# The heads stage: running maxima by broadcast loads, masks on the pool, and 32-row scores of four heads

## The reference, cut to what matters

```
log_f_cum = cumsum(log_sigmoid(fg))              # per head, along the sequence
log_D     = tril(log_f_cum[s] - log_f_cum[t]) + ig[t]      # -inf above the diagonal
D         = exp(log_D - max_t log_D)
C         = (q k^T / sqrt(32)) * D
h         = C / (max(|sum_t C|, exp(-max log_D)) + eps) @ v
out       = layernorm of h over each head's 32 features, times ln_scale
```

## Time and profile before

| | us |
|---|---|
| median of 3 runs | 1692.03 |
| lowest, highest | 1690.22, 1693.12 |
| the profiled execution's own time | 1693.99 |
| its span | 1692.3 |
| busy: TensorE, its weight loads, VectorE, ScalarE, pool | 1453.1, 1217.1, 922.0, 711.7, 357.9 |

### The profile page before, as it was taken

How to read it: one execution, slowest core, us unless ns; L and a number is a source line. 1 busy time by engine, 2 the same in 40 slices (tenths; PEclk the granted TensorE clock), 3 DMA queues, 4 the chain that set the end, 5 groups by cost and what they waited for, 6 DMA issues and landing times. The chain is left out here.

```text
span 1692.3 us, 27012 instructions
## 1 busy us (share of the span) xinstructions
PE 1453.1 (86%) x7570; PEld 1217.1 (72%) x7571; DVE 922.0 (54%) x1622; ACT 711.7 (42%) x1612; POOL 357.9 (21%) x253
## 2 busy tenths in 40 slices
PE   6999865998999996896999881499995899999977
PEld 5888732887888875775788650477885788888866
DVE  3222256558586877443444326733335977777774
ACT  3111134355555554512555541344444466666620
POOL 0111110104040310061862007111017900000004
PEclk8999988999999997698999995699996999999989
DMA  8763663954453543144664567732224455555402
GB/s 311 272 236 113 235 202 113 272 167 155 139 178 124 180 137 128 60 168 156 190 188 130 173 221 224 212 125 113 110 112 141 134 167 153 168 154 165 112 32 100
DMA packets 161503, 273.58 MB, mean 162 GB/s; under 512 B 28896, under 2 KB 63968, under 8 KB 157600
## 3 DMA queue, kind: packets, MB, share of 16 engines
q1 hardware_dynamic: 135920, 207.39, 38.7%
q10 hardware_dynamic: 17664, 38.68, 5.9%
q0 software_dynamic: 7856, 26.74, 4.7%
HBM read 162.00 MB, written 106.57 MB: 159 GB/s over the span
## 5 line engine op out<-in xcount | busy, mean ns | idle before, releaser
L2314 ACT ACTIVATE attend_prob<-banks,attend_row,rq 128x128 f32<-128x128 f32 x256 | 113.7, 454 | 70.1 <-DVE attend_row L2364 70.1
L1962 DVE TENSOR_TENSOR queries_total<-queries_total,queries_sq 128x512 f32<-128x512 f32 x64 | 44.3, 693 | 129.2 <-ACT queries_sq L1933 129.2
L100 PE MATMUL banks<-heads_split,heads_wl 128*128 (+1 forms) x256 | 109.4, 427 | 2.7 <-DVE heads_wt L744 2.7
L100 PE MATMUL banks<-of_x_lead,queries_wl 128*128 128x512 f32 x256 | 101.2, 395 | 7.7 <-ACT queries_sq L1933 4.4
L100 PE MATMUL banks<-attend_wol,attend_ol 128*128 (+1 forms) x256 | 106.7, 417 | 0.0
L100 PE MATMUL banks<-values_wl,of_ctx_lead 128*128 128x512 f32 x256 | 100.9, 394 | 4.3 <-DVE values_wt L2098 4.3
L101 PE MATMUL banks<-heads_split,heads_wl 128*128 (+1 forms) x256 | 103.0, 402 | 0.0
L102 PE MATMUL banks<-heads_split,heads_wt 128*128 (+1 forms) x256 | 102.6, 401 | 0.0
L102 PE MATMUL banks<-attend_wol,attend_ot 128*128 (+1 forms) x256 | 101.0, 395 | 0.0
L102 PE MATMUL banks<-of_x_lead,queries_wt 128*128 128x512 f32 x256 | 100.7, 393 | 0.0
L101 PE MATMUL banks<-attend_wot,attend_ol 128*128 (+1 forms) x256 | 100.7, 393 | 0.0
(11 more groups left out here) (306 smaller groups left out, 3880.7 us busy)
## 6 DMA issues: line engine op xcount, KB each, us to landing
v_heads<-values_out SPq DMA_DIRECT2D x16, 1024.0 KB, 4.8
heads_raw<-in_L_xattn_ki_w SPq DMA_DIRECT2D x32, 512.0 KB, 3.9
k_heads<-heads_key ACTq DMA_DIRECT2D x64, 256.0 KB, 3.1
q_heads<-queries_head ACTq DMA_DIRECT2D x16, 1024.0 KB, 3.9
attend_q<-q_heads SPq DMA_DIRECT2D x64, 256.0 KB, 4.1
of_attend_k<-k_heads SPq DMA_DIRECT2D x60, 256.0 KB, 4.0
of_attend_v<-v_heads SPq DMA_DIRECT2D x60, 256.0 KB, 3.3
sorted_rows<-values_zeros SPq DMA_DIRECT2D x2, 5120.0 KB, 19.9
```

The lines of the kernel that those rows point to most:

```text
L100: nc.tensor.matmul(out, lead_l, lead_r, start=first, stop=False)
L1962: nc.vector.tensor_tensor(t, t, sq[:, n % 2, :], ALU.add).then_inc(acc_done, 1)
L2314: ins = nc.scalar.activation(prob[:, j % 2, b, :], ps[:, j % 2, b * S:(b + 1) * S], ACT.Exp, bias=row[:, j % 2, 1, b:b + 1], scale=rq[:, b ...
```

## The change

- The running maxima g go to DRAM as they are made (four stores at the end of `gates`); the copy into `M.g` and the rest L328 are gone.
- In the heads stage SyncE loads g for two heads at a time, broadcast over the 128 partitions (`load_g`, 512 KB), into a ring of four. The pool writes 1e30 above the diagonal (`mask`), five units ahead. ScalarE's `exp` works out exp(a - g) by itself, four instructions of 128x128, each with a column of `M.nat` as bias. `maxima` and `argument` are gone, and with them `pick`, `far` and `ident_b`, `arg`, and two banks of PSUM.
- `qz` with its zeros (and their memset, L771) is replaced by `q`, one load for four heads. `scores` runs once in four steps, for four heads, each in its own 32 rows and its own bank.
- The pool's big steps are cut in four pieces each and placed between the masks; VectorE's two reductions and ScalarE's square are cut in two. ScalarE does `pair` first in a step, VectorE `decayed` first, TensorE `keys` first.

Core of the diff:

```diff
+            for g in range(G):                                   # gates, SyncE
+                sp.wait_ge(m_done, g + 1)
+                sp.dma_start(g_dram[g * H0 * N:(g + 1) * H0 * N].rearrange("(h n) -> h n", n=N),
+                             grow[0:H0, g * N:(g + 1) * N]).then_inc(g_stored, 16)
...
+            def load_g(g, k):
+                sp.dma_start(gmax[:, k % 4, :], g_dram[bass.ds((g * PAIRS + k) * 2 * N, 2 * N)]
+                             .partition_broadcast(P)).then_inc(g_ring[k % 4], 16)
+            load_g(0, 0), load_kT(0, 0), load_q(0, 0), load_g(0, 1), load_ctx(0)     # then kT, q,
+            ...                               # load_g(0, 2), load_g(0, 3), lnb, load_raw(0)
+            sp.wait_ge(qk, 4)
+            load_q(0, 2)                      # then load_split(0), load_raw(1), kbias, body(0)
...
+                    if n % 2 == 0:                               # body, SyncE
+                        sp.wait_ge(dec_done, g * PER + n + 2)
+                        load_g(g if k < PAIRS - 4 else after(g, PER)[0], (k + 4) % PAIRS)
...
+            def mask(g, n):                                      # pool
+                pool.wait_ge(g_ring[h // 2 % 4], (g * (PAIRS // 4) + n // 8 + 1) * 16)
+                nc.gpsimd.affine_select(out=t, in_=t, compare_op=ALU.is_ge, fill=FAR, base=0,
+                                        pattern=[[0, GB], [1, S]], channel_multiplier=-1).then_inc(masked, 1)
+            def body(g, first):
+                for n in range(PER):
+                    mask(g, n + AHEAD)
+                    if 5 <= n < 8: ...                           # pieces of values
+                        for at, step in ((3, centre), (8, scale), (10, weigh), (12, add)):
...
             def exp(g, n, first):                                # ScalarE
-                act.wait_ge(arg_done, g * PER + n + 1)
+                act.wait_ge(masked, g * PER + n + 1)
-                nc.scalar.activation(dec[:, n % 2], arg[:, n % 2], ACT.Exp).then_inc(dec_done, 1)
+                for b in range(GB):
+                    ins = nc.scalar.activation(dec[:, n % 2, b], gmax[...], ACT.Exp, scale=-1.0,
+                                               bias=M.nat[:, 0, bass.ds(g1, 1), b, h:h + 1]...)
+                ins.then_inc(dec_done, 1)
...
             def scores(g, n, first):                             # TensorE
-                nc.tensor.matmul(ps[:, 4 + n % 2, s], kT[:, c, s], qz[:, c % 2, j, s], ...)
+                if not (first and n < 4):
+                    pe.wait_ge(c_done, g * PER + n)
+                for b in range(GB):
+                    for j in range(4):
+                        ins = nc.tensor.matmul(ps[:, 2 + j, s], kT[r, c % C, s], q[r, c % 2, s], ...)
...
-                    maxima(g, n + 2, first)
-                    scores(g, n + 2, first)
                     lagging(g, n - LAG, keys)
+                    if n % 4 == 2:
+                        scores(g, n + 2, first)
                     outputs(g, n, first)
```

More of the change, by code:

```diff
@@ L375, in heads_and_keys @@
     LAG = 8
+    AHEAD = 5
     UNITS = PER * G
@@ new lines, in value @@
+            def value(g, count, b):
+                if b == 0:
+                    pool.wait_ge(loaded_ctx, (count + 1) * 16)
+                    if not isinstance(g, int) or g > 1:
+                        pool.wait_ge(pv, (count - 1) * PER)
+                    ph.hold(pool, held_pool)
+                ins = nc.gpsimd.tensor_copy(ctx1[:, bass.ds(half(g), 1), b, :, 0:DH0].rearrange("p a h e -> p (a h) e"),
+                                            ctx[:, b, :].rearrange("p (h e) -> p h e", e=DH0))
+                if b == GB - 1:
+                    ins.then_inc(ctx1_done, 1)
@@ new lines, in weigh, with add @@
+            def weigh(g, b):
+                if b == 0:
+                    pool.wait_ge(norm_done, FIRST + g + 1)
+                    ph.hold(pool, held_pool)
+                out = piece(sq, b).rearrange("p h e -> p (h e)")
+                ins = nc.gpsimd.tensor_tensor(out, out, lnb[:], ALU.mult)
+                if b == GB - 1:
+                    ins.then_inc(scale_done, 1)
+            def add(g, b):
+                if b == 0:
+                    pool.wait_ge(scale_done, g + 1)
+                    ph.hold(pool, held_pool)
+                xg = K.x[:, bass.ds(g * GB + b, 1), :].rearrange("p a d -> p (a d)")
+                ins = nc.gpsimd.tensor_tensor(xg, xg, piece(sq, b).rearrange("p h e -> p (h e)"), ALU.add)
+                if b == GB - 1:
+                    ins.then_inc(res_done, 1)
@@ new lines, in body @@
+            def body(g, first):
+                for n in range(PER):
+                    mask(g, n + AHEAD)
+                    if 5 <= n < 8:
+                        for b in ((0,), (1, 2), (3,))[n - 5]:
+                            value(after(g, PER)[0], g + 1, b)
+                    if not first:
+                        for at, step in ((3, centre), (8, scale), (10, weigh), (12, add)):
+                            if at <= n < at + 2:
+                                step(g - 1, 2 * (n - at))
+                                step(g - 1, 2 * (n - at) + 1)
@@ L571, in _ @@
+            for n in range(2):
+                mask(0, n)
+            for b in range(GB):
+                value(0, 0, b)
+            for n in range(2, AHEAD):
+                mask(0, n)
             nc.gpsimd.memset(total[:], 0.0).then_inc(total_blank, 1)
             pool.wait_ge(loaded_w, 16)
-            values(1, 1)
+            body(0, True)
             with pool.Fori(1, G) as g:
[L575 to L588, removed]
-                own(nc.gpsimd.tensor_tensor(out, out, lnb[:].unsqueeze(1).broadcast_to([P, GB, D]), ALU.mult))
-                xg = K.x[:, bass.ds((g - 1) * GB, GB), :]
-                nc.gpsimd.tensor_tensor(xg, xg, out, ALU.add).then_inc(res_done, 1)
@@ L658, in body @@
                 for n in range(PER):
-                    lagging(g, n - LAG + 1, weight_lead)
-                    exp(g, n + 2, first)
-                    lagging(g, n - LAG - 1, keep_key)
                     if n % 2 == 0:
@@ L666, in body @@
                             pair(g - 1, PAIRS - 1)
+                    lagging(g, n - LAG + 1, weight_lead)
+                    exp(g, n + 2, first)
+                    lagging(g, n - LAG - 1, keep_key)
                     if not first:
@@ L687, in _ @@
                 if m == PER - LAG + 3:
-                    square(last)
+                    square(last, 0)
+                    square(last, 1)
                 if m == PER - LAG + 6:
@@ L789, in _ @@
             finish(PER - LAG + 1)
-            mean(last)
+            mean(last, 0)
+            mean(last, 1)
             dve.wait_ge(mean_done, G)
-            shift(nc.vector, last)
+            for b in range(GB):
+                ins = shift(nc.vector, last, b)
+            ins.then_inc(centred, 1)
             for m in range(2, 5):
                 finish(PER - LAG + m)
-            variance(last)
+            variance(last, 0)
+            variance(last, 1)
             for m in range(5, 7):
```

253 lines of the change are left out of this document (122 added, 131 removed).

## The result

The changed kernel takes 1652.07 us (median of 4, 1649.65 to 1656.8) where the kernel before takes 1692.57 (4 runs): 0.9762 of it, 95% interval 0.9734 to 0.979. The forecast was 1644, its range 1622 to 1674. The profiled execution took 1652.70 us, its span is 1651.0.

What follows compares the result with a forecast made beforehand. TensorE was taken to bound the heads stage: 56 steps of 4.40 instead of 5.41 us (-56.6), a later start (+6.7) and loads catching up (+2) sum to -47.9, from 1693.99 to 1646.1, as a median 1644; range 1622 to 1674.

Steps and rivals of the forecast that it cites:

- TensorE bounds the stage; the step shrinks by what leaves it: Heads stage: TensorE sets the pace; its own step becomes 4.13 us, the whole step 4.40 instead of 5.41.
- Scores, 2.0 us for four heads: TensorE's scores in four row groups: half overlapped, 2.0 us per four heads, 0.55 a step with 0.05 for array shape changes.
- side by side in full: Rival on TensorE's scores: full overlap, TensorE 3.83, step 4.15, 14 us less, 1630; chance 0.10.
- The rest of the step: TensorE's step without scores: keys 2.66 and outputs 0.92 stay, 3.58 us; 0.05 for changing the array's shape.
- Stalls, 0.27 a step: Added to TensorE's 4.13 us step: table loads on ScalarE and collisions of pool, VectorE and loads, 4.3 us per 16 steps.
- ScalarE: ScalarE's step in the heads stage: four exponentials 1.14 us, 3.7 us of work in all, 85% busy, 10% under TensorE.
- ScalarE becomes the bound: Rival: four exponential instructions take 1.8 to 1.9 us, ScalarE 4.4, step 4.7, 17 us more, 1661; chance 0.18.
- VectorE and Pool: Heads stage: VectorE 2.9 us a step, pool 1.9, 0.4 charged for blocking; no 128x512 VectorE instruction above 2 us.
- DMA: Heads stage: broadcasts add 256 KB, 0.8 us a step; engines 3.4 of 4.4 us, share near 0.77.
- the 8 that would have sunk it: Sign against the forecast: broadcasts taking over 8 us to land in the steady part.
- Start: Start of keys in the heads stage: about 329 instead of 322.30, 6.7 us later, behind loads and the fifth broadcast.
- the loads that catch up in group 0: Group 0 of the heads stage: a further 2 us lost while loads catch up.

Runs made afterwards that it cites:

- the 1618 us kernel: Changed kernel with raw weights loaded ahead of ctx, the pair's copy last in ScalarE's step, and the group loop written out on four engines: 1618.40 us, ratio 0.956.
- the run from the same rows: The 1618 us kernel with the scores of all four heads taken from rows 0 to 31 instead of each head's own rows: 1710.13 us, ratio 0.9974.

## Why the prediction was right, step by step

- *TensorE bounds the stage; the step shrinks by what leaves it.* Right. The floor is 3.98 (forecast 4.13), and the 1618 us kernel, at 4.06, shows that it is one.
- *Scores, 2.0 us for four heads.* Too dear: 1.11. The rival "side by side in full" had it, and the run from the same rows shows the cause. The reason I gave for half, that the two passes of a matmul share their rows, didn't hold, as 1.11 us is near the 1.01 of full overlap; how the passes lie over each other no row shows. Worth 0.22 x 56 = 12 us, in the kernel's favour. The rest of the step was too cheap: 3.70 us where I had 3.58 and the 0.05 for changing the array's shape, for which I had no row. 4 us against.
- *Stalls, 0.27 a step.* This is the term that failed: 0.67, 22 us more. I priced table loads and collisions, but not ScalarE's order (`pair` first), nor raw's place behind 1 MB, nor the loop's turn. The three together are 287.00 - 254.54 = 32.5 us, 0.58 a step. Of the three, only raw's place is as it was before, where L635 waited for TensorE alone and never for the load. `pair` first is the change's own, and the trace of before has no stall at the turn. The disturbed steps that it does have, 4.75 and 3.19 us of idle TensorE the longest, are VectorE's behind Pool, and they went as forecast.
- *ScalarE.* Four exponentials take 1.26 to 1.28, forecast 1.14; its work is 175.59 / 240 x 4.65 = 3.40 a step, forecast 3.7, and it was 73% busy, not 85. The rival "ScalarE becomes the bound" is wrong as a sum of work: taking 0.56 us a step off it gave 1.3 us where nothing held it up. The four instructions for one did cost, by way of the hold-ups: with one instead, 20.8 us went, by lead or, at the turns, by shorter code.
- *VectorE and Pool.* Right: L797 fell from 1186 to 944 ns, and the whole Pool steps bring the long blocks back. No L797 took over 1.79 us. The masks do hold VectorE up, as the 1003 and 890 ns with and without them show, and were held up themselves (781 ns in the mean, 0.63 us the shortest); they cost the stretch nothing.
- *DMA.* Share 0.68 to 0.76 (forecast 0.77), a broadcast lands in 5.9 us at the median from 345 to 585, under the 8 that would have sunk it. That the traffic costs nothing was too kind: about 9 us, by way of raw and the turns.
- *Start.* Keys at 324.04, not 329. The fifth broadcast, blocked for 8.86 us on the queue, let the mask go at 320.46, near the early end of the 320 to 324 I gave to the loads alone: the queues ran at 342 GB/s and a share of 0.99 from 305 to 345, not at 260 to 300. 5 us in the kernel's favour.

In all, -12 for the scores, +4 for the rest of TensorE's step, -5 for the start, -2 for the loads that catch up in group 0 (they are inside the measured step) and +22 for the stalls: 7, where the profiled execution is 1652.7 - 1646.1 = 6.6 above the sum. That the forecast was so near is in part luck: the stalls were mis-sized by 22 us, and the other errors took 15 of them back.

## What to carry to other kernels

When the bounding engine's work shrinks, price next the once-a-group events of the engine that feeds it: a load behind a big one, whose lateness the longer step hid; an instruction placed so that it waits first; and the turn of a loop whose code has grown, which had cost nothing before. To tell whose stall an idle time is, see at which step of the group it stands and whether the last group has it too. A feeder at 73% can cost 20 us while it is held up and nothing when it isn't: test it again after the hold-ups are removed before rewriting its arithmetic. Small-row matmuls pay when neighbours in the order stand on different rows.

## What the runs showed of the hardware

- Sixteen fp32 matmuls of 32x128x128 take 1.11 us when neighbours are on different 32-row groups and 3.76 on the same one: 3.4 times. The Trainium skill, page "TensorE: Matmul & The Clock Gate", section "Measured speedup vs the span model", has 3.07 for four row tiles at 512 columns; here, at 128, it is no less.
- A run of 32-row matmuls on one row group cost clock: after 3.83 us of it the next matmuls started 0.43 us apart, the 1.2 GHz pace, after 1.11 us side by side 0.23.
- A loop's branch back can stop ScalarE for some 6 us, or not at all. Packets of one instruction queue (q14) from 345 to 585 are 5 before, 16 after, and 6 with one exponential instead of four; the turns cost TensorE nothing before and with one exponential. So in these three traces the turn has a cost where ScalarE's loop is longest and that queue moves most. Written out, the code takes 11 packets and has no stall at the turns. The Trainium skill, page "Runtime: NRT & Kernel Launch", section "Instruction fetch mechanics", says that a taken branch whose target is outside the two pages held has to fetch it first; the trace agrees as far as it goes, with two packets of that queue around each turn of the changed kernel and 13.9 us for writing the loop out. How much code is held no run shows.
- Chips differ in stages this change doesn't touch: 1694 against 1716 us for the same kernel, with keys stretches of 288.15, 287.00 and 287.91 us for the changed kernel twice and the one without masks, the last two on the chips of 1694 and 1715 us.
